# Inverses of the softmax sums: four columns on VectorE, widened by GpSimd, in place of 128 columns on VectorE

## The reference

```python
# scan, per batch: 512 channels, 16 states, 512 steps
state = state * exp(d_t * A) + (d_t * u_t) * B_t        # decay and input
y_t   = einsum('ben,bn->be', state, C_t)
x = x + tanh(g_xattn) * (y + D*u) * silu(z)
# attention on layernorm(x), per batch
scores = einsum('bqhd,bkhd->bhqk', q, k) * HEAD_DIM**-0.5    # causal mask follows
attn = softmax(scores)                                    # exp(s - max) / sum
ctx = einsum('bhqk,bkhd->bqhd', attn, v)
x = x + ctx @ wo
# then rms norm, router, top 2 of 8 experts, shared expert
```

## Time and profile before

| | |
|---|---|
| median of 3 executions | 1940.85 us (1940.26 to 1944.68) |
| profiled execution, its own time | 1938.13 us |
| its span, first to last instruction | 1936.3 us |
| TensorE busy | 1546.4 us, 80% |
| VectorE busy | 1221.5 us, 63% |
| ScalarE busy | 888.3 us, 46% |
| GpSimd busy | 786.2 us, 41% |
| mean granted TensorE clock | 0.853 |

### The profile page before, as it was taken

How to read it: one execution, slowest core, us unless ns; L and a number is a source line. 1 busy time by engine, 2 the same in 40 slices (tenths; PEclk the granted TensorE clock), 3 DMA queues, 4 the chain that set the end, 5 groups by cost and what they waited for, 6 DMA issues and landing times.

```text
span 1936.3 us, 26458 instructions
## 1 busy us (share of the span) xinstructions
PE 1546.4 (80%) x9104; PEld 1184.4 (61%) x9104; DVE 1221.5 (63%) x1730; ACT 888.3 (46%) x1973; POOL 786.2 (41%) x744
## 2 busy tenths in 40 slices
PE   5346877777957778767769676899999999999994
PEld 2234544455635555544547444778878899999973
DVE  4789669987488986599873452433232566656545
ACT  3433446664356662566642564121121466666510
POOL 0595145542255441355432021144321455555544
PEclk8555977888967788968889687999999999999997
DMA  5620001110101110001101111812120477777464
GB/s 192 235 77 22 23 11 33 55 45 27 40 22 50 53 36 28 11 28 55 45 23 66 55 34 50 347 63 101 60 71 1 183 251 263 244 252 258 156 234 157
DMA packets 92372, 191.54 MB, mean 99 GB/s; under 512 B 8704, under 2 KB 25600, under 8 KB 88912
## 3 DMA queue, kind: packets, MB, share of 16 engines
q1 hardware_dynamic: 87120, 173.07, 26.0%
q0 software_dynamic: 5120, 16.78, 2.6%
HBM read 136.21 MB, written 53.61 MB: 98 GB/s over the span
## 4 chain that ended last, share of the span: by engine, by line
PE 40%; DVE 6%; issue 5%; ACT 3%; POOL 3%; DMA 0%; DVEq 0%; ACTq 0%; SPq 0%; POOLq 0%
PE scores L526 21%; PE bank L526 12%; DVE HS L1370 2%; POOL yab L1924 2%; PE scores L645 1%; DVE YA L1380 1%; PE bank L673 1%; PE bank L658 1%; PE bank L823 1%; PE bank L590 1%; ACT EX L1035 1%; ACT PT L1043 1%; ACT bank L1000 1%; DVE nm L1422 1%; POOL lal L1917 1%
## 5 line engine op out<-in xcount | busy, mean ns | idle before, releaser
L1781 POOL TENSOR_TENSOR GB<-DU,BB 128x512 f32<-128x512 f32 x256 | 327.4, 1292 | 138.8 <-DVE HS L1370 83.4
L590 PE MATMUL bank<-ident,HS 128*128 128x128 f32 x896 | 190.8, 351 | 181.0 <-DVE YA L1380 126.4
L1370 DVE TENSOR_TENSOR_SCAN HS<-bank,GB 128x512 f32<-128x512 f32 x224 | 270.4, 1207 | 33.7 <-ACT bank L1000 15.5
L590 PEld LDWEIGHTS bank<-ident,HS 128*128 128x128 f32 x896 | 128.7, 176 | 231.8 <-DVE YA L1380 167.2
L1000 ACT ACTIVATE bank<-DL,aneg 128x512 f32<-128x512 f32 x224 | 155.0, 692 | 139.3 <-DVE HS L1370 138.0
L1380 DVE SCALAR_TENSOR_TENSOR YA<-bank,Ct,YA 128x512 f32<-128x512 f32 x224 | 164.8, 736 | 27.5 <-PE bank L590 25.2
L526 PE MATMUL scores<-xth,wgh 128*128 128x256 f32 x552 | 158.0, 286 | 2.0 <-DVE fa L1667 1.1
L1043 ACT ACTIVATE PT<-bank 128x128 f32<-128x128 f32 (+3 forms) x256 | 110.3, 431 | 107.2 <-PE bank L658 106.2
L526 PE MATMUL scores<-xth,wgl 128*128 128x256 f32 x552 | 156.1, 283 | 0.0
L526 PE MATMUL scores<-xtl,wgh 128*128 128x256 f32 x552 | 156.0, 283 | 0.0
L658 PE MATMUL bank<-ident,EX 128*128 128x128 f32 x640 | 132.5, 316 | 26.5 <-ACT PT L1043 24.9
(11 more groups left out here) (241 smaller groups left out, 3816.4 us busy)
## 6 DMA issues: line engine op xcount, KB each, us to landing
wgr<-wffn_in SPq DMA_DIRECT2D x108, 384.0 KB, 6.5
wdr<-wffn_in SPq DMA_DIRECT2D x81, 256.0 KB, 3.2
BB<-b_scratch SPq DMA_DIRECT2D x64, 256.0 KB, 3.2
xg<-V SPq DMA_DIRECT2D x1, 11776.0 KB, 39.2
xr<-xg SPq DMA_DIRECT2D x23, 512.0 KB, 5.7
yg<-ysb SPq DMA_DIRECT2D x23, 512.0 KB, 6.4
hah<-hhd SPq DMA_DIRECT2D x5, 1024.0 KB, 6.0
hal<-hhd SPq DMA_DIRECT2D x5, 1024.0 KB, 8.0
```

The lines of the kernel that those rows point to most:

```text
L590: mm = nc.tensor.transpose(state_bank(s, q)[:, et * P:(et + 1) * P], HS[:, n % 2, et, tt * P:(tt + 1) * P], ident[:])
L1370: nc.vector.tensor_tensor_scan(HS[:, n % 2, et, :], decay_bank(s, k), GB[:, k % 4, :], 0.0, ALU.mult, ALU.add).then_inc(scan_done, 1)
L1781: nc.gpsimd.tensor_tensor(GB[:, k % 4, :], DU[:, et, :], BB[:, n % 2, :], ALU.mult).then_inc(gb_ready, 1)
```

## The change

The inverse is now taken of the four sums alone, into a new small tile `ri`, and GpSimd multiplies the four inverses, each repeated 32 times, by a row of ones, which gives the same `rib`. A new semaphore `rw_done` counts the widened inverses; `weigh` waits for it in place of `ri_done`. The reuse of `rib` is now guarded on GpSimd (by `pv_mm`), the reuse of `ri` on VectorE (by `rw_done`). On GpSimd `widen` stands in iteration q behind `driven` 4q+3 and ahead of `ctl` of q-1. The row of ones takes one more small memset at the start, and the semaphore for the zero tile is merged with that of the rows of constants.

```diff
+        ri = mid("ri", [P, 2, HG])
...
             def weigh(b, q):
                 i, m = quad(q)
                 pe.wait_ge(pt_done, UN * b + HG * (q + 1))
-                pe.wait_ge(ri_done, NQ * b + q + 1)
+                pe.wait_ge(rw_done, NQ * b + q + 1)
...
             def invert(b, q):
                 dve.wait_ge(ex_done, UN * b + HG * (q + 1))
-                at(dve, pv_mm, NQ * b + q - 1)
-                nc.vector.reciprocal(rib[:, q % 2], rs[:, q % 2].unsqueeze(2).broadcast_to([P, HG, HD])
-                                     ).then_inc(ri_done, 1)
+                at(dve, rw_done, NQ * b + q - 1)
+                nc.vector.reciprocal(ri[:, q % 2], rs[:, q % 2]).then_inc(ri_done, 1)
...
+            def widen(b, q):
+                pool.wait_ge(ri_done, NQ * b + q + 1)
+                at(pool, pv_mm, NQ * b + q - 1)
+                nc.gpsimd.tensor_tensor(rib[:, q % 2], ri[:, q % 2].unsqueeze(2).broadcast_to([P, HG, HD]),
+                                        one[:].unsqueeze(2).broadcast_to([P, HG, HD]), ALU.mult).then_inc(rw_done, 1)
...
                     for a in range(2):
                         if scn and k + a < NB:
                             driven(s, k + a)
+                    if att:
+                        widen(b, q)
                     if att and q:
                         context(b, q - 1)
...
-            for row, value in ((mhalf, -0.5), (eps5, 1e-5), (eps6, 1e-6), (mone, -1.0), (perh, 1.0 / H)):
+            for row, value in ((mhalf, -0.5), (eps5, 1e-5), (eps6, 1e-6), (mone, -1.0), (perh, 1.0 / H),
+                               (one, 1.0)):
                 nc.gpsimd.memset(row[:], value).then_inc(rows_made, 1)
-            pool.wait_ge(rows_made, 5)
-            nc.gpsimd.memset(V[:, 0, :], 0.0).then_inc(zt_made, 1)
+            pool.wait_ge(rows_made, 6)
+            nc.gpsimd.memset(V[:, 0, :], 0.0).then_inc(rows_made, 1)
```

More of the change, by code:

```diff
@@ L72, in build @@
         tgq = keep("tgq", [P, 1])
-        mhalf, eps5, eps6, mone, perh = [keep(n, [P, T4]) for n in ("mhalf", "eps5", "eps6", "mone", "perh")]
+        mhalf, eps5, eps6, mone, perh, one = [keep(n, [P, T4]) for n in ("mhalf", "eps5", "eps6", "mone", "perh", "one")]
         tick = keep("tick", [P, 1])
@@ L253, in build @@
         s_mm, mx_done, ex_done = sem("scores_ready"), sem("row_max"), sem("exp_ready")
-        ri_done, rb_done, cn_done = sem("row_sum_inverse"), sem("inverse_turned"), sem("context_normed")
+        ri_done, rw_done = sem("row_sum_inverse"), sem("inverse_widened")
+        rb_done, cn_done = sem("inverse_turned"), sem("context_normed")
         t_mm, pt_done, pv_mm = sem("probs_transposed"), sem("probs_copied"), sem("pv_ready")
@@ L262, in build @@
         h2_st, hh_st = sem("h2_rows_stored"), sem("h2_parts_stored")
-        zt_made, zfill = sem("zeros_made"), sem("slots_zeroed")
+        zfill = sem("slots_zeroed")
         hh_ld = [sem(f"h2_parts_loaded{b}") for b in range(B)]
@@ L390, in begin_attention @@
                     load_x(1, i)
-                sp.wait_ge(zt_made, 1)
+                sp.wait_ge(rows_made, 7)
                 sp.dma_start(xg.rearrange("(n p) h -> p n h", p=P),
```

## The result

The changed kernel takes 1933.72 us (median of 14 executions, 1931.83 to 1935.96), the kernel before 1942.56 us (median of 14, 1934.9 to 1948.67). The ratio is 0.9955, 95% interval 0.9943 to 0.9967: 8.8 us or 0.45% faster. Forecast were 15.8 us, 0.8%. The direction was right and the time lies inside the range; the gain is little over half of what was summed up. The profiled execution of the changed kernel took 1934.3 us with a span of 1932.5. That is close to its median, while the profiled execution before (1938.13) was one of the quicker ones. So the two spans differ by 3.8 us only, and the comparison of traces is one of places, not of totals.

The account below looks back on a forecast made before the run. VectorE, busy 92% of the woven loops, was taken as the bound, with decays and scores close behind. Handover gains of 10.9 + 2.2 + 1.6 + 0.7 + 0.4 = 15.8 us gave 1922.3 us (1925.0 on the median's footing), range 1911 to 1937.

Parts of the forecast that it names:

- The decay as the next limit: In the woven loops, the next scan waits for ScalarE's decay, so scans follow no closer than 2.04 us.
- handover: Stretch between the add_state behind scan 4q+3 and scan 4q+4, where the inverse stands; 48 in three loops, 2.63 us scan-to-scan.
- free handover: Handover where scores leave the row maximum room, so only the decay limits: 0.59 us gain each, 18 places, 10.9 us.
- What comes next: the scores: Row maximum of q+1 waits for TensorE's scores, whose chain does not move with the inverse; without room the gain is lost.
- list of 48: All woven-loop handovers, each gaining the smallest of 0.77 us, room behind the decay and room behind the scores: 15.8 us.
- the 13 held ones: Handovers in the woven loops where the row maximum already lacks room behind TensorE's scores: together 0.4 us gain.
- the late decays: Five handovers at q = 14, 15 where ScalarE, busy with a step of finish, starts the decay late: 1.6 us gain.
- the last attention loop: Its 16 inverses lie inside time TensorE weighs and makes the next scores: no gain taken, bound 12 us.
- The freed time is mostly given back: Rival, chance 0.18: in the woven loops TensorE at a lower granted clock removes the rooms; 1933 or about 1937 us.
- Its first case: All three woven loops run at clock 0.75, two losing 4 us each: a gain of 7.8, 1933 us; rival's chance 0.18.
- VectorE is the only pace: Rival, chance 0.13: in the woven loops TensorE's and ScalarE's chains move along, freeing 37 us, to 1904 us.
- The collision of VectorE and GpSimd: Rival, chance 0.05: each GpSimd widening stretches overlapping VectorE work; with all 0.45 us of it, 1954 us.

Follow-up runs that it names:

- one behind a wide inverse: Kernel before, keeping the inverse over 128 columns, with GpSimd then multiplying those columns by ones in place: 1945.43 us against 1944.2, ratio 1.0005.
- an inverse of 345 ns: Changed kernel with VectorE's inverse over 32 columns instead of four, GpSimd copying them to the other 96: 1933.67 us, ratio 0.9953 to the kernel before.
- the pair without the mask: Kernel before and changed kernel, each without the four small matmuls that add the causal mask to the scores: 1936.18 us and 1917.32 us.
- the early turn: Transposition of rib moved from the weighing's head to ahead of the last turned head, 7 of 16 iterations: 1936.42 us on kernel before, 1924.08 on changed.
- the filler: Four needless transpositions on TensorE ahead of each weighing: 1935.46 us in the changed kernel, 1939.22 us in the kernel before.

## Why the prediction was wrong

- **The prices of the parts** were right: 170 ns for the inverse where 180 were told, 410 ns for a widening where 454 were told, and nothing for it on any path (three widenings cost no more than one, and one behind a wide inverse costs nothing).
- **The decay as the next limit** was right. A handover is 2.08 us where 2.04 was told, VectorE waits 74 times for the decay in place of 55, and an inverse of 345 ns is as good as one of 170.
- **The size of a free handover** was 0.49 to 0.51 and not 0.59: 0.04 from the handover, 0.06 from the scan behind it, which showed 1.22 us in place of 1.16 once it was no longer close behind another instruction. Over eleven places that is 1 us. (The list's 10.9 is 17 x 0.59 + 0.76 = 10.8 by its own terms, which changes nothing.)
- **The step that failed** is "What comes next: the scores", in its list of 48. It took the room ahead of each row maximum as the one trace showed it, and kept TensorE's chain fixed. In fact 18 free handovers were counted for 10.9 us where eleven gave their 0.5 and all 18 gave 5.7, and the 13 held ones and the late decays, which were to bring 2.0 us, lost 1.4: VectorE's waits for scores grew by 10.4 us in place of at most 8. Part of this was in the rows already. Three places (q = 6, 7, 10) were free in one round of three, the one in which they met the higher clock, and I booked them as gains: there the chain from the weighing to the mask took 1.62, 1.84 and 2.10 us at a clock of 0.97 to 1.00, in the other rounds 2.30 to 3.56 us at 0.50 to 0.55, and after the change 2.74, 2.99 and 3.65 us. The list also left out the add_state behind the maximum, which cost the three places at q = 2 most of their gain.
- **Why TensorE was late** is shown in part. At q = 14 the same matmuls ran at a granted clock of 0.60 in place of 0.98. An estimate from this pair of traces, taking at each held maximum the smaller of its new wait and of what its chain, the same matmuls, grew by: 5.7 us of the 10.4 by which the waits grew are chains that ran longer, at q = 10, 12 and 14 above all; the rest is VectorE coming earlier to the same chain. That a shorter TensorE chain makes the change worth more is shown by the pair without the mask, 18.9 us in place of 8.8, and so above the 15.8 of the forecast. The other pairs fit it, but less surely: 12.3 with the early turn (1936.42 - 1924.08) is within the intervals of 8.8, and 24.1 with both goes in part with the clock. Why TensorE met the lower clock more often after the change stays open: the filler raised the clock and did not settle it.
- **The footing.** The sum was made against one profiled execution whose own time lies 4.4 us under the later median of the kernel before. By the three loops alone the change brings 6.3 us from first to last inverse (163.54, 167.75 and 163.35 before; 163.34, 163.53 and 161.44 after), where some 5 us each were told; the last attention loop took 111.46 and takes 111.37. The medians say 8.8. The kernel before has the wider spread (1934.9 to 1948.67 against 1931.83 to 1935.96), and its 58 executions beside the experiments with a clock of 0.849 to 0.853, where the changed kernel's lie, have a median of 1944.1 us. So the one trace from which the room was read was a favourable one, and how much the change is worth depends on the executions that it is held against.
- **The rivals.** "The freed time is mostly given back" at 0.18 came closest in kind, by the mechanism named there: TensorE at a lower granted clock. Its first case even has the number, 1933 for 1933.7 measured, but in part by luck: it had all three loops at 0.75, and they ran at 0.76 to 0.77. "VectorE is the only pace" fell with the kernel that has no inverse at all (1932 us, not 1904). The collision of VectorE and GpSimd did not come in the changed kernel; it came in the experiment with a copy on VectorE. The last attention loop gained nothing, as told.

The warning of the Trainium skill's page GPSIMD Engine Reference, section Engine selection, against elementwise work on GpSimd holds for the instruction and not for this place. A 128x128 widening takes 410 ns on GpSimd, as a multiplication, and 226 ns as an undisturbed copy on VectorE; but on GpSimd it lies in the 6 us of room ahead of its use, while the copy took 693 ns at the median in the woven loops and cost the whole gain.

## What to carry to other kernels

When an instruction on the busiest engine gets cheaper, go place by place and ask which wait ends next; here the answer was the decay in eleven of 48 places and TensorE's scores in most of the others, and an inverse of 345 ns was as good as none at all, within the intervals. Treat a room that another engine leaves as uncertain when that engine's clock moves, above all if it shows in one repetition of three. And once the limit has a name, shorten that chain: turning the widened inverses ahead of the weighing brought 9.6 us more by the medians, as much as the change itself.

## What was not expected of the hardware

A copy of 4 numbers to 128 columns on VectorE, from SBUF to SBUF, took between 226 and 1353 ns in the woven loops, where GpSimd multiplies most of the time, and 226 or 227 ns in all 16 places of the last attention loop, where nothing ran on GpSimd beside it. The long ones end with GpSimd's instruction. Two rows of the run with the widening on VectorE:

```profile
609.47 0.70 DVE L1431 COPY rib<-ri 128x128 f32<-128x128 f32 x1
```

```profile
608.79 1.30 POOL L1785 TENSOR_TENSOR GB<-DU,BB 128x512 f32<-128x512 f32 x1 [0.77 <-DVE HS L1372]
```

The copy ends at 610.17, 0.08 us after the multiplication (610.09). So it is in the loops wherever the copy took longer than 0.23 us and the 128x512 instruction beside it stands alone in the timeline: 0.07 to 0.10 us after its end. The scans of the same run, which read PSUM and one SBUF tile, kept to between 1203 and 1225 ns. The Trainium skill's page GPSIMD Engine Reference, section Specifications, names VectorE's 2-port modes among the cases in contention with GpSimd; the copy's spread agrees, though no run here shows which mode it ran in.

Taking work from TensorE can bring nothing. Against the kernel before that each was compared with, the early turn brings 8.5 us, leaving out the mask 8.0, and both together 1.5 (1940.03 us), with a median granted clock over all their executions of 0.852, 0.848 and 0.841. Why the clock is lower with both is not shown.
